# Local attention with exponentials held in PSUM, four-tile value products, and a state space scan one channel half at a time

## The reference, cut to what matters

```python
def local_attention(q, k, v):           # 16 heads of 64, windows of 32 tokens
    ...
    bk2, bv2 = (look(bk), look(bv))     # each window sees itself and the one before
    sim = jnp.einsum('bhwie,bhwje->bhwij', bq, bk2) * QK_SCALE      # 8.0
    sim = jnp.where(mask, -jnp.finfo(sim.dtype).max, sim)
    attn = jax.nn.softmax(sim, -1)
    out = jnp.einsum('bhwij,bhwje->bhwie', attn, bv2)

for i in range(DEPTH):                  # 6
    x = attn_layer(shift_tokens(x), Wqkv[i], q_scale[i], k_scale[i], Wo[i]) + x
    x = ffn_layer(shift_tokens(x), ln_g[i], ln_b[i], W1[i], b1[i], W2[i], b2[i]) + x

def step(h, inp):                       # state space: 256 channels, 16 states, 256 steps
    d_t, x_t, B_t, C_t = inp
    A_bar = jnp.exp(d_t[:, :, None] * A)
    h = A_bar * h + (d_t * x_t)[:, :, None] * B_t[:, None, :]
    y_t = jnp.einsum('bdn,bn->bd', h, C_t)
    return (h, y_t)
```

## Time and profile before

| | |
|---|---|
| median of 2 runs | 2734.66 us (2733.21 and 2736.12) |
| profiled execution, time | 2734.42 us |
| profiled execution, span | 2732.6 us |
| mean granted clock of TensorE | 0.948 of full speed |
| busy: TensorE, VectorE, ScalarE, GpSimd | 2391.9, 2401.9, 1988.0, 1164.5 us |
| steady stretch of the attention, 1000 to 1500 us | TensorE 475.8, VectorE 469.4, ScalarE 420.3, GpSimd 226.4 us |

### The profile page before, as it was taken

The page is one execution under the profiler, slowest core; times in us unless marked ns, Lnnn a source line. Parts: engine busy times, 40 slices in busy tenths (PEclk is TensorE's granted clock), DMA queues, the critical chain, the costliest instruction groups (busy, mean ns, idle before and its releaser), DMA issues. The chain is left out here.

```text
span 2732.6 us, 60708 instructions
## 1 busy us (share of the span) xinstructions
PE 2391.9 (88%) x23660; PEld 1246.6 (46%) x23660; DVE 2401.9 (88%) x2594; ACT 1988.0 (73%) x3169; POOL 1164.5 (43%) x465
## 2 busy tenths in 40 slices
PE   7789999999999999999999999999998765565778
PEld 2345555555555555555555555555554222122355
DVE  5799999999999999999999999999995799999542
ACT  4778888888888888888888888888886643333433
POOL 0444444444444444444444444444441066566130
PEclk8899999999999999999999999999999877678889
DMA  0100000000000000000000000000000100000001
GB/s 20 52 2 2 2 24 10 10 2 2 24 10 10 2 13 13 9 10 2 13 13 14 5 2 13 13 17 2 2 2 1 36 0 0 0 0 0 17 16 46
DMA packets 15995, 29.49 MB, mean 11 GB/s; under 512 B 3616, under 2 KB 6064, under 8 KB 15664
## 3 DMA queue, kind: packets, MB, share of 16 engines
q1 hardware_dynamic: 15760, 25.78, 3.0%
HBM read 24.73 MB, written 1.05 MB: 9 GB/s over the span
## 5 line engine op out<-in xcount | busy, mean ns | idle before, releaser
L705 POOL TENSOR_TENSOR f_rot<-f_raw,f_tabc 128x1024 f32<-128x1024 f32 x192 | 453.0, 2360 | 925.3 <-DVE f_qk L753 583.6
L709 POOL TENSOR_TENSOR f_rot<-f_rot,f_shuf 128x1024 f32<-128x1024 f32 x192 | 452.4, 2356 | 235.6 <-DVE f_shuf L746 235.6
L746 DVE TENSOR_TENSOR f_shuf<-f_shuf,f_tabs 128x1024 f32<-128x1024 f32 x192 | 427.9, 2229 | 8.6
L776 DVE TENSOR_TENSOR f_s<-f_s,f_rcp 128x512 f32<-128x512 f32 x192 | 401.5, 2091 | 6.6
L604 ACT ACTIVATE f_raw<-f_ps 128x1024 f32<-128x1024 f32 x192 | 196.0, 1021 | 227.3 <-PE f_ps L425 227.3
L472 PEld LDWEIGHTS f_ps<-f_ptz,f_v 64*64 64x64 f32 x6144 | 259.1, 133 | 146.9 <-issue 146.9
L1133 POOL TENSOR_TENSOR s_prod<-s_state,s_cs 128x1024 f32<-128x1024 f32 x64 | 234.1, 3677 | 169.4 <-DVE s_state L1211 142.3
L968 PE MATMUL s_ps<-s_prod,s_ident 128*128 128x512 f32 x256 | 183.0, 872 | 132.7 <-POOL s_prod L1133 132.7
L595 ACT ACTIVATE f_v<-f_ps 64x256 f32<-64x256 f32 x768 | 287.0, 374 | 6.7
L472 PE MATMUL f_ps<-f_ptz,f_v 64*64 64x96 f32 (+1 forms) x6144 | 285.4, 243 | 2.3 <-ACT f_ptz L625 2.3
L424 PE MATMUL f_ps<-f_xs,f_wq 128*128 128x512 f32 x384 | 211.8, 633 | 71.1 <-ACT f_rn L613 47.1
(11 more groups left out here) (266 smaller groups left out, 3961.3 us busy)
## 6 DMA issues: line engine op xcount, KB each, us to landing
e_w<-in_e_w SPq DMA_DIRECT2D x16, 256.0 KB, 2.8
f_wq<-in_f_wq SPq DMA_DIRECT2D x12, 256.0 KB, 2.6
f_wk<-in_f_wk SPq DMA_DIRECT2D x12, 256.0 KB, 3.4
f_wv<-in_f_wv SPq DMA_DIRECT2D x12, 256.0 KB, 3.6
f_wo<-in_f_wo SPq DMA_DIRECT2D x6, 512.0 KB, 3.3
f_w<-in_f_w SPq DMA_DIRECT2D x6, 341.0 KB, 2.9
s_dx<-in_k_pick SPq DMA_DIRECT2D x1, 1536.0 KB, 9.1
f_w<-in_f_w SPq DMA_DIRECT2D x6, 192.0 KB, 3.2
```

The lines of the kernel that those rows point to most:

```text
L705: pool.tensor_tensor(view(rot, 0, [S, 4], [1, S]), view(raw, 0, [S, 4], [1, S]), view(tab_c, 0, [S, 2], [0, 2], [1, S]), ALU.mult).then_in ...
L709: pool.tensor_tensor(rot[:, :], rot[:, :], shuf[:, :], ALU.add).then_inc(sem["rot"], 1)
L746: dve.tensor_tensor(view(shuf, 0, [S, 4], [1, S]), view(shuf, 0, [S, 4], [1, S]), view(tab_s, 0, [S, 2], [0, 2], [1, S]), ALU.mult).then_i ...
L776: dve.tensor_tensor(view(t, 0, [64, 8], [1, 64]), view(t, 0, [64, 8], [1, 64]), view(rc, 0, [1, 8], [0, 64]), ALU.mult).then_inc(sem["p"], 1)
```

## The change

In the attention, the exponentials are written by ScalarE into banks 4 and 5 of PSUM in place of the tile `s`; the sum and the final product of `soft_b` read them there, and that product writes the probabilities to `s`. `scores(j)` waits for `p` (the end of `soft_b(j-1)`) in place of `shift`. The value product of a pair of 64-token groups is made as four products of 64 stationary columns (tokens) by 256 moving ones (value channels), with the even heads on partitions 0 to 63 and the odd ones on 64 to 127, so that one ScalarE copy replaces four.

In the state space, the loop is over four blocks (token half h, channel group k), each with 16 states; B and C are spread again for each block. The drive reads B from PSUM (banks 4 and 5), the decay is written by ScalarE to PSUM (banks 2 and 3, one buffer) and read there by the scan, C is still copied to SBUF, and the sums stand in banks 0 and 1. The gate product of a block is done after the second drive of the next one. The memset of the decay's first columns moves from GpSimd to VectorE.

```diff
             def values(i, q):
...
-                pe.matmul(bank(2), xs[:, 128 * (q % 4):128 * (q % 4) + 128], wv[:, CH * (q // 4):CH * (q // 4) + CH],
-                          start=True, stop=True).then_inc(sem["v_mm"], 1)
+                for r in range(2):
+                    for h in range(2):
+                        at = 128 * (q % 4) + 64 * r
+                        mm = pe.matmul(view(ps, 2 * CH + 256 * r, [1, 256], p0=64 * h, rows=64), xs[:, at:at + 64],
+                                       view(wv, CH * (q // 4) + 64 * h, [128, 4], [1, 64]),
+                                       start=(r == 0), stop=True, skip_group_check=True)
+                mm.then_inc(sem["v_mm"], 1)
...
             def scores(i, j):
                 gather(sem["qk"], i * 8 + j + 1)
-                gather(sem["shift"], i * 8 + j)
+                gather(sem["p"], i * 8 + j)
...
-                for r in range(2):
-                    for h in range(2):
-                        ins = act.activation(view(v, (2 * (q % 4) + r) * CH + 256 * (q // 4), [64, 4], [1, 64], p0=64 * h, rows=64),
-                                             view(ps, 2 * CH + 64 * h, [128, 4], [1, 64], p0=64 * r, rows=64), ACT.Copy)
-                ins.then_inc(sem["v"], 1)
+                act.activation(view(v, 2 * (q % 4) * CH + 256 * (q // 4), [CH, 2], [1, 256]),
+                               view(ps, 2 * CH, [256, 2], [1, 256]), ACT.Copy).then_inc(sem["v"], 1)
...
-                    act.activation(s[j % 2][:, :], s[j % 2][:, :], ACT.Exp, scale=8.0).then_inc(sem["exp"], 1)
+                    act.activation(view(ps, 4 * CH, [CH, 2], [64, 4], [1, 64]), view(s[j % 2], 0, [64, 2], [128, 4], [1, 64]),
+                                   ACT.Exp, scale=8.0).then_inc(sem["exp"], 1)
...
-                dve.tensor_reduce(sm[:, :], view(t, 0, [64, 8], [1, 64]), AX.X, ALU.add).then_inc(sem["sum"], 1)
+                dve.tensor_reduce(view(sm, 0, [4, 2], [1, 4]), view(ps, 4 * CH, [CH, 2], [64, 4], [1, 64]), AX.X,
+                                  ALU.add).then_inc(sem["sum"], 1)
...
-                dve.tensor_tensor(view(t, 0, [64, 8], [1, 64]), view(t, 0, [64, 8], [1, 64]), view(rc, 0, [1, 8], [0, 64]),
-                                  ALU.mult).then_inc(sem["p"], 1)
+                dve.tensor_tensor(view(t, 0, [64, 2], [128, 4], [1, 64]), view(ps, 4 * CH, [CH, 2], [64, 4], [1, 64]),
+                                  view(rc, 0, [4, 2], [1, 4], [0, 64]), ALU.mult).then_inc(sem["p"], 1)
...
+            def spread(h, i, n):
+                need(pe, sem["drive"], i)
+                for c in range(2):
+                    mm = pe.matmul(bank(BB + c), pick[:, bass.ds(n * C, C)],
+                                   parts[:, h * H + c * CH:h * H + c * CH + CH], start=True, stop=True)
+                mm.then_inc(sem["b_mm"], 1)
+                need(pe, sem["c_in"], i)
...
+            def add(i, par, first=False):
+                pe.wait_ge(sem["prod"], i + 1)
...
+                with pe.Fori(1, DS // 2 - 1) as n2:
+                    for par in range(2):
+                        spread(h, n2 * 2 + (base + par + 1), n2 * 2 + (par + 1))
+                        add(n2 * 2 + (base + par - 1), 1 - par)
...
+            def step(h, k, i, n, par):
+                need(act, sem["scan"], i)
+                act.activation(view(ps, DB * CH + 1, [S, B // 2], [1, S - 1]),
+                               view(delta, k * T + h * H + 1, [S, B // 2], [1, S - 1]),
+                               ACT.Exp, scale=aneg[:, bass.ds(n, 1)]).then_inc(sem["decay"], 1)
+                act.wait_ge(sem["c_mm"], i + 1)
+                need(act, sem["prod"], i - 1)
+                act.activation(view(cs[par], 0, [1, H]), view(ps, CB * CH, [1, H]), ACT.Copy).then_inc(sem["c_in"], 1)
...
+            def step(i, par):
+                pool.wait_ge(sem["scan"], i + 1)
+                pool.wait_ge(sem["c_in"], i + 1)
+                need(pool, sem["acc"], i - 1)
+                pool.tensor_tensor(prod[par][:, :], st[par][:, :], cs[par][:, :], ALU.mult).then_inc(sem["prod"], 1)
...
+            def drive(h, k, i, par):
+                dve.wait_ge(sem["b_mm"], i + 1)
+                need(dve, sem["prod"], i - 1)
+                dve.tensor_tensor(st[par][:, :], dx[:, k * T + h * H:k * T + h * H + H], view(ps, BB * CH, [1, H]),
+                                  ALU.mult).then_inc(sem["drive"], 1)
+            def scan(i, par):
+                dve.wait_ge(sem["drive"], i + 1)
+                dve.wait_ge(sem["decay"], i + 1)
+                dve.tensor_tensor_scan(st[par][:, :], view(ps, DB * CH, [1, H]), st[par][:, :], 0.0, ALU.mult,
+                                       ALU.add).then_inc(sem["scan"], 1)
```

More of the change, by code:

```diff
@@ L883, in state_space @@
         pick = m.mem.enter_context(nc.sbuf_tensor("s_pick", [96, 2 * DS * C], BF16))
[L885 to L887 removed]
+        st, prod, cs = ([m.sb(f"s_{n}{par}", T // 2) for par in range(2)] for n in ("state", "prod", "cs"))
         ident = m.sb("s_ident", C)
@@ L893, in state_space @@
             "load pick left_mm left conv xl right_mm gate dpre_mm dpre dabs dexp dlog bc_mm bc split "
-            "a_in a0 a1 a2 zero dx fin b_mm c_mm b_in c_in decay drive scan prod acc seen gated mean cen sq var lv rstd nrm aff o_mm o").split()}
+            "a_in a0 a1 a2 zero dx fin b_mm c_mm c_in decay drive scan prod acc gated mean cen sq var lv rstd nrm aff o_mm o").split()}
         loads = [(wl[:, :], io["s_wl"]), (wr[:, :], io["s_wr"]), (cols[:, :], io["s_cols"]), (wd[:, :], io["s_wd"]),
@@ L902, in state_space @@
         added = m.sem("s_added")
-        D0, D1 = 2 * K, 2
+        BLOCKS = [(h, k) for h in range(2) for k in range(K)]
+        YB, DB, BB, CB = 0, 2, 4, 6
         body = ExitStack()
@@ L950, in _ @@
             pe.wait_ge(sem["gate"], 2 * NCH)
[L952 to L970, removed]
+            def spread(h, i, n):
[5 more added lines that the diff above has]
+                need(pe, sem["c_in"], i)
+                for c in range(2):
+                    mm = pe.matmul(bank(CB + c), pick[:, bass.ds((n + DS) * C, C)],
+                                   parts[:, h * H + c * CH:h * H + c * CH + CH], start=True, stop=True)
+                mm.then_inc(sem["c_mm"], 1)
+            def add(i, par, first=False):
+                pe.wait_ge(sem["prod"], i + 1)
+                for c in range(2):
+                    mm = pe.matmul(bank(YB + c), ident[:, :], prod[par][:, c * CH:c * CH + CH],
+                                   start=first, stop=True, skip_group_check=True)
+                mm.then_inc(sem["acc"], 1)
             def mean(c):
@@ L975, in mean @@
                 mm.then_inc(sem["mean"], 1)
[L977 to L985, removed]
-                    for par in range(2):
[L987 to L990, removed]
+            pe.wait_ge(sem["split"], 12)
+            spread(0, 0, 0)
+            for b, (h, k) in enumerate(BLOCKS):
+                base = b * DS
+                spread(h, base + 1, 1)
+                if b:
+                    add(base - 1, 1)
+                    pe.wait_ge(sem["gated"], b)
+                spread(h, base + 2, 2)
+                add(base, 0, first=True)
+                with pe.Fori(1, DS // 2 - 1) as n2:
+                    for par in range(2):
+                        spread(h, n2 * 2 + (base + par + 1), n2 * 2 + (par + 1))
+                        add(n2 * 2 + (base + par - 1), 1 - par)
+                spread(h, base + DS - 1, DS - 1)
+                add(base + DS - 3, 1)
+                if b + 1 < len(BLOCKS):
+                    if b == 1:
+                        pe.wait_ge(sem["split"], 24)
+                    spread(BLOCKS[b + 1][0], base + DS, 0)
+                else:
+                    pe.wait_ge(sem["drive"], base + DS)
                     mean(0)
                     mean(1)
-                add(h, DS - 2, 0)
-                add(h, DS - 1, 1)
-            pe.wait_ge(sem["c_in"], 2 * DS + D1)
+                add(base + DS - 2, 0)
+            add(len(BLOCKS) * DS - 1, 1)
+            pe.wait_ge(sem["c_in"], len(BLOCKS) * DS)
             pe.wait_ge(sem["gated"], 2 * K)
```

103 lines of the change are left out of this document (39 added, 64 removed).

## The result

| | before | after |
|---|---|---|
| median of 2 runs | 2734.66 us | 2913.23 us (2911.21 and 2915.25) |
| ratio, with its 95% interval | | 1.0653, 1.0607 to 1.0699 |
| span of the profiled execution | 2732.6 us | 2913.5 us |
| a unit of eight slots in the attention | 83.3 us | 95.6 us |

The change costs 178.6 us. The forecast was 2784 and its range ended at 2855.

A forecast was written before the change was run, and what follows sets the result against it. In attention TensorE (95% busy, full of work) and VectorE (94%, partly waiting for GpSimd) were both taken as near the limit. 2734.4 + 140 (slot loop) + 12 (clock) - 102 (state space) = 2784 us, range 2700 to 2855.

The forecast's parts named there:

- The sign: Whole kernel: which way the time moves; chances given were faster 0.10, same 0.44, slower 0.46.
- the term of the clock: Attention, slots 6 and 7: TensorE's idle time halves its clock in one unit in six, 12 us more.
- The ring: Attention: `scores(j+1)` waits for `p(j)`, closing a loop through TensorE's and VectorE's queues each slot; 140 us more.
- the gate products: Attention, slot 5: if they hold it and every release takes 0.2 us, the added cost reaches 8 us a unit.
- L776: Last product of `soft_b` on VectorE: 2.10 to 0.69 us with one operand in PSUM, 1.41 us a slot.
- The values: Attention's value product as four, overlapped in pairs: 0.2 us for two more shape changes, on the path in slots 0, 1, 7.
- the rival in which the tiles don't overlap: Value products in attention: 0.86 us more in slots 0, 1 and 7, 74 us in all, 2858 us; chance 8%.
- The four value copies: ScalarE in attention: four copies become one; costed at nothing, as only `raw_copy`, ahead of them, was on the path.
- The state space: State space stage: 64 cycles of 3.74 us, 341 to 239 us, a gain of 102 us; bounds 60 and 112.
- two releases: State space cycle: hand-overs around the single decay buffer, taken as 0.33 us together beside scan 2.27 and decay 1.14.
- The rival that named this mechanism: Attention, slots 6 and 7: TensorE's clock halves in nearly every unit, 57 us more, 2841 us; chance 17%.

The follow-up runs named there:

- exponentials alone: Kernel before with exponentials in PSUM banks 4 and 5 and scores waiting for `p`; values and state space as before: 2986.17 us, ratio 1.0917.
- the wait alone: Kernel before with one line changed, scores waiting for `p` instead of `shift`, operands staying in SBUF: 3251.59 us, ratio 1.1892.

## Why the prediction was wrong in size

The sign and the mechanism were right, the term of the clock was not. Point by point:

**The ring** holds. With the clock at 1.00 the unit is 89.63 us; the prediction had 89.6 by the slots, then 89.4. Slots 2, 3 and 4 came within 0.1 us. Slot 6 (13.64 for 14.0), slot 7 (14.02 for 14.4) and slots 0 and 1 are 0.1 to 0.4 shorter. Slot 5 is 1.1 longer, and the sum hides both: that it came out to 0.03 is partly luck. What holds slot 5 is in VectorE's timeline of the kernel after:

```profile
1194.20 0.69 DVE L827 TENSOR_TENSOR f_xn<-f_cen,f_sq 128x512 f32<-128x512 f32 x1 [2.35 <-ACT f_sq L679]
1194.81 0.68 DVE L764 TENSOR_REDUCE f_max<-f_ps 128x8 f32<-128x512 f32 x1
```

An operation of the feed-forward part waits for ScalarE's reciprocal root, and `soft_a` stands behind it in the queue. Before, there was slack for that; on the ring it is late. I had named the gate products as what could hold slot 5. Before, that slot took 10.60 (masks at 1222.09 and 1232.69) with 0.94 of waits in it; the forecast's 9.6 had no room for any.

**L776** went to 0.69, as taken, and the wait for GpSimd is gone. **The values** cost 0.18 us of TensorE's time on the ring: query product to `mix` is 2.93 (1193.23 to 1196.16), where it was 2.75. Eight records of 256 columns lie in 1.08 us, where the old product's two of 512 took 1.02 to 1.06, so the rival in which the tiles don't overlap falls. The Trainium skill, "TensorEngine Tiling (Array Packing)", "Key Properties", says that changing the tiling mode drains the TensorE; the prediction's estimate of what that would cost was 0.44 us, and 0.18 was measured, nearer to its 0.2. The four value copies were not free on the ring: slot 5 is 11.75 with them (exponentials alone) and 10.68 with one copy, so their going gave 1.1 us a unit that I had costed at nothing. Alone, the value change costs 64 us, by the stall at the loop's start and the clock behind it. The prediction had no term for that; that the kernel after doesn't show the stall was luck.

**The state space** gained 110 us, where the sum had 102: 3.63 us a cycle for 3.74. (The prediction's two releases, 0.08 and 0.22, make 0.30 and not 0.33, so its sum should have read 3.71.) The Trainium skill, "SBUF — State Buffer", "Who interferes with whom", says that a VectorE instruction with at most one SBUF input doesn't contend with GpSimd. A scan agrees here: L1213 with one operand in PSUM takes 2.29 us with GpSimd's L1135 at work, and L1135 takes 2.37 on average, where the same product took 3.68 before, beside drives and scans with both inputs in SBUF.

**The clock** is the step that failed: "One unit in six so hit, 3 us each, gives 12 us; bounds 0 and 69." The runs showed every unit of the steady stretch hit, in slots 7 and 0 both: 95.57 - 89.63 = 5.9 us a unit, 23 x 5.9 = 137 us. My price of 3 us counted three slow query products. But the ring leads through everything that TensorE does between two masks until the clock is back, in two slots. And I took the chance of a fall from one row with an idle time of 3.31 us, beside which 2.9 looked mild. The rival that named this mechanism was right in kind and was given 17% and 57 us. Its bound of 69 was 23 x 3, so the range was too narrow by the same price.

The account: -110 (state space, measured alone), +145 (the ring, 23 x 6.3), +137 (the clock, 23 x 5.9) make +172, and 178.6 was measured; the 6 us between stay open. Giving TensorE work in the gaps returned 114 of the 137; in that kernel some units still have a slot 3 of 11.2 instead of 9.5 us, or a slot 0 of 10.7 to 11.2.

**Interaction.** The exponentials alone (+251) and the state space alone (-110) add to 2876; with the values it is 2913. The 37 us are not the stall in the scores, which the kernel after doesn't show. They are the clock: with the values every unit falls, without them every other one, with a smaller fall in slot 3 in the units between. The average unit there is 93.9 us (95.9 and 91.9), 1.7 less than 95.57, and 23 x 1.7 = 39. The clock's own part is larger: at full clock that unit would be 90.2 (91.87 less the 1.64 of slot 3) against 89.63, so the falls take 3.6 us there and 5.9 here, and the shorter ring gives 0.6 back. Why the value change tips each unit and not each second one is open.

## What to carry to other kernels

A buffer that is held until a later step has read it turns two loosely coupled queues into a ring: add it up over one period from the in-order queues, and look in the ring for an operation that can stand behind the release, as `soft_b` ahead of the sine's product did here (279 us, the clock's falls in slots 7 and 0 among them). Where the ring leaves the busiest engine a few idle microseconds once a period, price the clock for every period and for all the work until it is back, or show that it holds. And before shortening a busy engine's operations, ask if they are long because they wait: taking 81 of 469 us from VectorE was worth 13 us, while TensorE stayed busy 478 of 500.

## What the runs showed of the hardware

**The granted clock fell behind short waits.** Waits of 2.87 and 2.61 us, once a unit and one slot apart, brought it down in all units of the kernel after from 500 to 2000 us, to 0.51 in the stretch shown. In the kernel with the exponentials alone waits of 2.91 and 2.60 did so in every second unit, and in the units between the clock fell in slot 3, behind a wait of 1.72: it is 0.85 from 1341.30 to 1352.40, and that slot takes 11.15 us instead of 9.51. With 1.16 us in place of 2.87 it stayed at 1.00 through slots 7 and 0. The same kernel shows how little the length settles: ahead of slot 3 TensorE waits 1.56 us in every unit, as in the kernel after; there the clock never fell behind it, here it did in some units (0.85 and 11.2 us from 666.08). Behind the stalls of 1.2 to 2.3 us in slot 0 it fell to 0.88 or 0.78 over the slot in more than half of the units and stayed at 1.00 in the others. With the wait alone, slot 3 from 557.26 us kept 1.00 behind a wait of 3.20, and slot 3 from 660.41, behind 3.19, had 0.87.

**A longer loop body can stall TensorE at the loop's start.** Six more records a slot, of the value products or of products whose result is thrown away, bring to the kernel before a stall of 1.2 to 2.3 us once a unit; with the clock that falls behind it the two kernels lose 64 and 67 us. It shows in the profile as "issue" in the scores, and the instruction queue carries 240 packets for 218. The kernel after has the packets without the stall. That TensorE waits there for its instructions to arrive is argued from the place and the packets, not seen by itself. The Trainium skill, "Runtime: NRT & Kernel Launch", "Instruction fetch mechanics", says that a taken branch to a target outside the window of instructions already fetched must wait for a DMA; this case's place and its packets agree, and no run here shows the size of the window.
